# A four-layer decoder on one core: the last layer's expert loads reordered, and its combine written into the experts' block

## The reference, cut to what matters

```python
probs = jax.nn.softmax(xr @ Wg, axis=-1)               # 4096 tokens, 8 experts
gate_vals, expert_idx = jax.lax.top_k(probs, 2)
# at most C = 1280 tokens to an expert, in token order; what is over is dropped
dispatched = xr[...].reshape(E, C, d)                  # rows of each expert's tokens
h = jax.nn.relu(jnp.einsum('ecd,edf->ecf', dispatched, w1))     # 256 -> 1024
expert_out = jnp.einsum('ecf,efd->ecd', h, w2)                  # 1024 -> 256
out = jnp.einsum('ks,ksm->sm', combine_weights, rerouted)       # two experts of each token
...
x = x + jnp.tanh(g_ffn[3]) * _L3_ffn_ref(_layernorm(x, axis=-1), L3_ffn_Wg, L3_ffn_w1, L3_ffn_w2)
return x
```

## Time and profile before

| | us |
|---|---|
| timed runs, median of 3 | 3621.99 |
| timed runs, lowest and highest | 3617.33, 3624.50 |
| the profiled execution | 3609.43 |
| its span, first to last instruction | 3607.7 |
| experts of the last layer, first pair turned to last copy | about 2938 to 3547 |
| first load of the combine to the end | 3558.6 to 3607.7 |

### The profile page before, as it was taken

One profiled execution on the slowest core, in us unless ns is written; L12 is line 12 of the kernel. 1 busy time (PEld: TensorE's weight loads), 2 busy tenths in 40 slices (PEclk: granted clock), 3 DMA queues, 4 the chain that ended last, 5 costly groups with the idle time before them and its releaser, 6 DMA issues. The chain is left out here.

```text
span 3607.7 us, 60300 instructions
## 1 busy us (share of the span) xinstructions
PE 2864.7 (79%) x20178; PEld 1832.3 (51%) x20178; DVE 2156.4 (60%) x4946; ACT 1479.5 (41%) x3032; POOL 1108.2 (31%) x1494
## 2 busy tenths in 40 slices
PE   5488886366899994589847798999889649999993
PEld 4233334122455553433323585444478648888882
DVE  7699994677677775634578686888777610000003
ACT  5377773254222224589835453222255211111120
POOL 3211110377233335412298441000044431111110
PEclk7599996698999997599969899999999669999996
DMA  8766643499422223688300440000044221112104
GB/s 272 195 114 119 120 105 140 151 371 356 138 80 82 77 82 132 166 136 137 59 1 1 160 145 27 1 1 1 1 160 133 96 60 56 47 53 79 60 29 140
DMA packets 261417, 386.10 MB, mean 107 GB/s; under 512 B 56673, under 2 KB 188750, under 8 KB 260864
## 3 DMA queue, kind: packets, MB, share of 16 engines
q1 hardware_dynamic: 230288, 305.68, 31.6%
q0 software_dynamic: 25152, 68.22, 5.4%
q10 hardware_dynamic: 5680, 8.39, 0.7%
HBM read 227.49 MB, written 160.24 MB: 107 GB/s over the span
## 5 line engine op out<-in xcount | busy, mean ns | idle before, releaser
L3172 POOL DMA_INDIRECT rows_out<-e_out,e_tr_dest x224 | 234.8, 1048 | 867.3 <-DVE e_out L3822 506.4
L3822 DVE COPY e_out<-e_psD 128x512 f32<-128x512 f32 x40 | 27.7, 692 | 495.4 <-PE e_psD L3790 495.2
L1243 ACT ACTIVATE a_pt<-a_psS 128x512 f32<-128x512 f32 x512 | 277.6, 595 | 107.9 <-PE a_psS L1139 103.5
L3584 PE MATMUL e_psG<-e_wgu,e_yT 128*128 x576 | 277.8, 605 | 29.3 <-ACT e_yT L3616 26.7
L1265 DVE TENSOR_REDUCE a_mx_sb<-a_psM 128x4 f32<-128x1024 f32 x256 | 293.2, 1215 | 12.3 <-PE a_psM L1122 11.4
L1153 PE MATMUL a_psV<-a_pt,a_vt 128*18 128x256 f32 x4096 | 291.2, 386 | 2.6 <-issue 2.1
L3790 PE MATMUL e_psD<-e_w,e_hT 128*128 128x256 f32 x1280 | 291.8, 388 | 0.0
L3779 PE MATMUL e_psH<-e_yT,e_w 128*128 128x256 f32 x1280 | 284.5, 381 | 1.6 <-issue 0.8
L3722 ACT ACTIVATE e_hT<-e_psH 128x512 f32<-128x512 f32 x160 | 95.5, 597 | 454.0 <-PE e_psH L3779 454.0
L3790 PEld LDWEIGHTS e_psD<-e_w,e_hT 128*128 128x128 f32 x1280 | 247.2, 196 | 33.7
L3779 PEld LDWEIGHTS e_psH<-e_yT,e_w 128*128 128x128 f32 x1280 | 244.2, 191 | 35.6 <-issue 2.1
(11 more groups left out here) (433 smaller groups left out, 6126.0 us busy)
## 6 DMA issues: line engine op xcount, KB each, us to landing
kbd<-e_wd SPq DMA_DIRECT2D x64, 512.0 KB, 3.8
cr_kbd<-kbd SPq DMA_DIRECT2D x64, 512.0 KB, 3.6
rows_in<-zeros POOLq DMA_DIRECT2D x36, 522.0 KB, 6.5
e_xin<-rows_in SPq DMA_DIRECT2D x144, 128.0 KB
vbd<-e_bd SPq DMA_DIRECT2D x64, 272.0 KB, 3.9
cr_vbd<-vbd SPq DMA_DIRECT2D x64, 272.0 KB, 2.7
cq_rows<-rows_out SPq DMA_DIRECT2D x32, 512.0 KB, 6.0
e_w<-in_L_ffn_w_dram SPq DMA_DIRECT2D x16, 1024.0 KB, 7.6
```

Source lines behind the costliest of these rows:

```text
L1243: act.activation(pt[:, probs(t, h), b, :, :], psS[:, unit(t, h, b) % S_BANKS, :].rearrange("p (k c) -> p k c", k=KC), ACT.Exp, scale=scale ...
L3172: pool.indirect_dma_start(out=self.rows_out[0:limit, :], out_offset=bass.IndirectOffsetOnAxis(ap=self.dest[:, t:t + 1], axis=0), in_=rows, ...
L3584: ins = pe.matmul(psG[:, u, :], yT[:, u, k, :], wgu[:, e, k, :], start=(k == 0), stop=(k == KC - 1))
```

## The change

Two things change, both in the last layer's feed-forward part.

SyncE's list in `phase_experts3` now loads the rows of pair `i` and only then looks whether pair `i - 3` was the last of an expert and its weights are to be replaced. The buffers and the waits of each load stay as they are.

The combine is no longer a block of its own: its steps stand at the end of the engines' lists in the experts' block. SyncE waits until all scatters have landed and then loads the rows, now into eight buffers, which lie in `hT`, the space of the experts' hidden values. VectorE adds them as before. The stores go out by ScalarE's queue, 16 of two tiles each (256 KB) in place of eight of four tiles. `phase_combine` is removed, and the context that held the experts' weights is kept open to the end.

```diff
-                def pair(j, last):
-                    for g in range(NG):
-                        if g + 2 < NG:
-                            load(j, g + 2)
-                        elif not last:
-                            load(j + 1, g + 2 - NG)
-                        if not last and g % GR == GR - 1:
-                            spent(j, g)
-                            weights(j + 1, g // GR)
-
-                load(0, 0)
-                load(0, 1)
-                for j in range(E // 2):
-                    pair(j, j == E // 2 - 1)
+                for i in range(E * GR):
+                    load(i // NG, i % NG)
+                    done = i - 3
+                    if done >= 0 and done % GR == GR - 1 and done // GR + 2 < E:
+                        spent(done // NG, done % NG)
+                        weights(done // NG + 1, done % NG // GR)
+                for u in range(2):
+                    sp.wait_ge(stored[u], 32 * (E * GR // 2))
+                for t in range(TILES):
+                    if t >= BUFS:
+                        sp.wait_ge(combined, t - BUFS + 1)
+                    sp.dma_start(rows[:, t % BUFS, :, :], chosen[t]).then_inc(got[t % BUFS], 16)
...
+    BUFS, GROUP, K = 8, 2, 2
...
+        rows = hT[:, :, :, :].rearrange("p u f c -> p (u f c)").rearrange("p (b k d) -> p b k d", b=BUFS, k=K)
...
                 run(act, step)
+                for g in range(0, TILES, GROUP):
+                    act.wait_ge(combined, g + GROUP)
+                    act.dma_start(result[:, g:g + GROUP, :], core.xs[:, g:g + GROUP, :]).then_inc(finished, 16)
+                act.wait_ge(finished, 16 * (TILES // GROUP))
...
                 run(dve, step)
+                for t in range(0, TILES, 2):
+                    for v in range(2):
+                        dve.wait_ge(got[(t + v) % BUFS], ((t + v) // BUFS + 1) * 16)
+                        dve.scalar_tensor_tensor(out=core.xs[:, t + v, :], in0=rows[:, (t + v) % BUFS, 0, :], scalar=weight[:, t + v, 0:1],
+                                                 in1=core.xs[:, t + v, :], op0=ALU.mult, op1=ALU.add).then_inc(added, 1)
+                    for v in range(2):
+                        dve.wait_ge(added, t + v + 1)
+                        dve.scalar_tensor_tensor(out=core.xs[:, t + v, :], in0=rows[:, (t + v) % BUFS, 1, :], scalar=weight[:, t + v, 1:2],
+                                                 in1=core.xs[:, t + v, :], op0=ALU.mult, op1=ALU.add).then_inc(combined, 1)
```

More of the change, by code:

```diff
@@ L3173, in send @@
                                 in_=rows, in_offset=None, bounds_check=limit - 1, oob_is_err=False).then_inc(stored, 16)
[L3176 to L3232, removed]
@@ L3667, in _, with phase_experts3 @@
                                                  op0=ALU.mult, op1=ALU.add).then_inc(out_ready, 1)
-def phase_experts3(core, rows_in, rows_out, w1, w2, w1s, w2s, w_loaded):
+def phase_experts3(core, rows_in, rows_out, w1, w2, w1s, w2s, w_loaded, weight, result):
     nc = core.nc
@@ L3680, in phase_experts3 @@
     stored = [core.lasting_sem(f"{n}s{u}") for u in range(2)]
+    BUFS, GROUP, K = 8, 2, 2
+    got = [core.sem(f"{n}g{u}") for u in range(BUFS)]
+    added, combined, finished = (core.sem(n + k) for k in ("add", "com", "fin"))
+    chosen = rows_out[0:TILES * P * K, :].rearrange("(t p k) d -> t p k d", p=P, k=K)
     x_turned, x_copied, up_done, relued, down_done, out_ready = (core.sem(n + k) for k in ("xt", "xc", "up", "re", "down", "out"))
@@ L3907, in flamingo_decoder @@
             weight = core.sb(c, "weight3", [P, TILES, 2], F32)
[L3908 to L3912, removed]
+            weights, prefetch = expert_weights3(core, c, a["L3_ffn_w1"], a["L3_ffn_w2"])
+            phase_route_scatter(core, a["L3_ffn_Wg"], weight, rows_in, 8 * CAPACITY, MARK3, f_gate(3), prefetch)
+            phase_experts3(core, tiles_in, rows_out, a["L3_ffn_w1"], a["L3_ffn_w2"], *weights, weight,
+                           out.rearrange("b s d -> (b s) d").rearrange("(t p) d -> p t d", p=P))
 _INS = ['x', 'ctx_2048', 'g_xattn', 'g_ffn', 'L0_ffn_router_weight', 'L0_ffn_router_bias',
```

## The result

| | kernel before | changed kernel |
|---|---|---|
| timed runs, median of 4 | 3623.24 us | 3570.01 us |
| lowest and highest | 3617.33, 3628.54 | 3567.41, 3573.89 |
| the profiled execution | 3609.43 us | 3567.41 us |
| ratio of the timed runs | | 0.9856, 95% interval 0.9841 to 0.9870 |

A forecast was written before the change was run, and what follows sets the result against it. TensorE was taken to set the experts' pace, losing 34.0 us at six late row loads; 34.0 + 7.0 (hand-over) + 5.0 (combine) = 46.0 us off 3621.99 gave 3576 us, range 3565 to 3591.

The forecast's parts named there:

- Loads ahead: Layer 3's experts: rows loaded before the weights remove six TensorE stalls and the lower clock behind them, 34.0 us gained.
- load 8's 10 us to spare: Experts' stage: pair 8's rows, now behind the weights, are due 20 us after issue; slowest landing 9.2 us, no new wait.
- Hand-over: Between experts and combine: without a block end, the first load no longer waits for GpSimd's drain, 7.0 us gained.
- Combine: Last stage: eight buffers and stores by ScalarE's queue bring it from 49.1 to 44.1 us, 5.0 us gained.
- Step 3: The prediction's part on the combine: only the buffers fill 10.3 us without transfers; ScalarE's queue alone at most 3 us.
- The second term: Combine: 5.3 us without transfers at its start and end, added to 38.8 us of transfers.
- Rival B: Combine falls to VectorE's pace, 36.8 us in all, 12 us off; total 3569 us; chance 0.12.
- The weighed rule: Combine: the skill's HBM limit of about 358 GB/s gives 35.1 us of transfers; set aside for the rows' mean, 324 GB/s.
- A: Combine gains nothing, forecast holds for the rest; total 3581 us; chance 0.14.
- C: Experts' stage: a new wait at pair 8's rows or the tags takes back 17 us; total 3593 us; chance 0.05.
- D: Experts' stage: the gate of pair 7's load is still closed, so the stall stays; total 3610 us; chance 0.03.
- E: Experts' stage: without pauses TensorE's clock falls, making the kernel slower, about 3726 us in one case; chance 0.02.

The follow-up runs named there:

- wait_first: Changed kernel, but SyncE waits for the spent weights before loading the rows, and the weights follow the rows; experts' stage 546.97 us.
- filled_pause: Changed kernel with the old order of loads, TensorE turning the identity 32 times in each of six pauses; experts' stage 571.17 us.
- own_block: Changed kernel with the combine in a second block behind the experts' one; ratio 0.9864, 11.92 us from last copy to first load.

## Why the prediction was right where it was, and wrong in one term

**Loads ahead: right, by its own steps.** 34.0 us forecast, 33.9 measured. Load 7's place behind the weights was the cause (wait_first), the excess over the waits was the clock (filled_pause), and load 8's 10 us to spare are real (none lost at 4 MB, six waits at 8 MB). One sum on the way was loose: 7.07 + 0.60 + 7.07 + 7.07 is 21.8 and not 21.6, and the turn of pair 8 came at T+20.95, since the blocks overlap a little at their ends (a beat takes 14.25 us, its three parts add up to 14.74). The 10 us stay: 20.95 - 1.64 - 9.4 = 9.9.

**Hand-over: right.** 7.0 us, 6.6 of them the drain (own_block).

**Combine: the mechanism right, the size wrong.** Step 3 said that only the buffers can fill the idle time; they did. But it reckoned 38.8 us of transfers and 5.3 us without any, 44.1 in all, and 37.3 came out: 0.94 x 37.3 = 35.1 us busy and 2.2 us idle. So by this count both terms were mis-sized (by 3.7 and 3.1 us). As the share reads up to 1.06, the split between them is rough; their sum is not. The first took the rate while busy of the kernel before, 324 GB/s, for a constant of the transfers. It isn't one. The rate while busy is 250 / 0.82 = 305 GB/s with four buffers in the new place, 337 / 0.94 = 359 with eight and 355 / 0.99 = 359 with the stores in SyncE's queue; in the steady part near 400 GB/s are moved. Why a packet of a shallow pipeline takes longer was not tried. The second term added the ends to the transfers as if nothing moved in them, while stores of earlier tiles fill part of them.

Rival B had the size, 12 us off, and nearly the sum (37.3 for its 36.8), but not the reason; that they agree is luck. VectorE still waits for rows, 12.1 us in all, of which 6.9 up to the first (before: 28.1 and 13.9), and the DMA engines set the pace. Nor are B's 1.91 us for four additions VectorE's own pace. Where sixteen buffers hold rows ready for it, it does four in 1.58 us:

```profile
3542.54 0.88 DVE L3779 SCALAR_TENSOR_TENSOR xs<-e_rows,weight,xs 128x256 f32<-128x256 f32 x2
3543.33 0.88 DVE L3783 SCALAR_TENSOR_TENSOR xs<-e_rows,weight,xs 128x256 f32<-128x256 f32 x2
3544.12 0.88 DVE L3779 SCALAR_TENSOR_TENSOR xs<-e_rows,weight,xs 128x256 f32<-128x256 f32 x2
```

With that, B's sum would have been 16 x 1.58 + 2.6 + 3.6 = 31.5 us. I gave B 0.12 because 400 GB/s stood in one slice only; that slice was the rate which the engines reach when they are fed, and it was the better guide than the mean.

**The weighed rule.** The Trainium skill (DMA: Bandwidth & Descriptors, section Where 436 GB/s comes from) puts a core's limit at the HBM at about 358 GB/s. The trace doesn't agree: 392 GB/s over 26 us, two bytes read to one written. Here the measurement decides. That the rule's 35.1 us of transfers equal the 35.1 of the trace is a coincidence of a slow start and a faster steady part.

**The rivals.** A (no gain in the combine) is refuted by the traces of all eight-buffer kernels. C and D would show as waits of TensorE behind the first; there is none. E needed a lower clock without a pause: TensorE worked 500 us on end at 1.00.

**The total.** The sum came to 52.6 us for 46.0, all of the difference in the one term (6.8 us too little gained, 0.1 the other way). The forecast median is 6 us high for the same reason; it would be 7, had the median of the kernel before not moved up by 1.2 us with its fourth run.

## What to carry to other kernels

In a queue that feeds both small urgent and large patient transfers, issue the urgent one first; what it waits behind counts in bytes ahead of it, and the consumer's pause can cost more than its length, when the clock falls in it (here half as much again, summed over six pauses). Before two blocks are left apart, look for the drain between them. And don't take the rate while busy of a shallow pipeline of transfers as what the engines can do: here the fullest slice said more than the mean, and the number of buffers was worth 13 us, the issuing queue nothing.

## What the runs showed of the hardware that was not expected

- The rate while busy of the same transfers rose from about 305 to 359 GB/s with the depth alone, and the traffic stood at 391 to 406 GB/s in the steady part with reads and writes mixed. In the changed kernel's first 7 us most slices show only 233 to 308 GB/s; why was not tried.
- GpSimd's drain behind these scatters took 6587 ns in all fourteen traces, at whatever time it began; at the end of other blocks of the same program it took 5292, 2748, 1370 and 46 ns. What sets its length was not tried.
- The stages ahead of the last layer's experts, the same in all kernels, put its first copy anywhere from 2964.9 to 2980.5 us in fourteen traces, while the experts' stage itself repeats within 0.02 us where it has no waits, and the combine within 1 us. A difference of 10 us between two profiled executions is no evidence here; cut by stage, the same traces settle 1 us.
